# Cross-attention: the key and query fills for two batches ahead open an iteration, and the normalised input is turned one iteration earlier, at the end

## What is computed

```python
x = x + _L0_attn_ref(_layernorm(x), wq, wk, wv, wo)
# cross-attention, 16 heads of 16
q = _split_heads(_layernorm(x) @ Wq.T + bq)
k = _split_heads(ctx @ Wk.T + bk)
v = _split_heads(ctx @ Wv.T + bv)
scores = jnp.where(mask == 0, -jnp.inf, einsum('bhqd,bhkd->bhqk', q, k) / 4)
x = x + (merge(softmax(scores) @ v) @ Wo.T + bo)
x = x + _L0_ffn_ref(_layernorm(x), ...)
```

## Time and profile before

| | |
|---|---|
| median of 3 runs | 1809.52 us (1806.7 to 1829.16) |
| the profiled execution | 1793.75 us, of which its span 1791.8 us |
| mean granted TensorE clock of it | 0.924 |
| TensorE busy | 1543.1 us (86% of the span) |
| VectorE, ScalarE, GpSimd busy | 1053.8, 765.4, 427.1 us |
| the steps of the cross-attention | about 782 to 1375 us of the span |

### The profile page before, as it was taken

The page is one execution under the profiler, slowest core; times in us unless marked ns, Lnnn a source line. Parts: engine busy times, 40 slices in busy tenths (PEclk is TensorE's granted clock), DMA queues, the critical chain, the costliest instruction groups (busy, mean ns, idle before and its releaser), DMA issues. The chain is left out here.

```text
span 1791.8 us, 39290 instructions
## 1 busy us (share of the span) xinstructions
PE 1543.1 (86%) x12244; PEld 1335.2 (75%) x12244; DVE 1053.8 (59%) x2627; ACT 765.4 (43%) x1830; POOL 427.1 (24%) x564
## 2 busy tenths in 40 slices
PE   4799999999999999379889898989988606999998
PEld 3687878788888888367778787878876605888886
DVE  5658575767676666256566665666654314555553
ACT  4546464545555554135455554555543101222221
POOL 4202020202020303411222222222212062333332
PEclk9899999999999999679899998999886557999999
DMA  5603030302021111285666666566651052555552
GB/s 192 167 1 75 1 73 3 70 13 61 23 50 34 39 39 35 67 212 144 162 174 168 173 169 165 148 177 165 168 138 57 1 162 82 173 174 174 190 186 62
DMA packets 159949, 195.71 MB, mean 109 GB/s; under 512 B 83724, under 2 KB 128307, under 8 KB 159636
## 3 DMA queue, kind: packets, MB, share of 16 engines
q1 hardware_dynamic: 154356, 186.09, 38.1%
q0 software_dynamic: 3968, 6.59, 1.1%
q10 hardware_dynamic: 1568, 2.30, 0.4%
HBM read 138.63 MB, written 58.05 MB: 110 GB/s over the span
## 5 line engine op out<-in xcount | busy, mean ns | idle before, releaser
L1197 DVE TENSOR_REDUCE row_max<-psb_s 100x1 f32<-100x361 f32 x512 | 264.7, 531 | 201.8 <-PE psb_s L1340 200.1
L1090 ACT ACTIVATE probs<-psb_t 121x400 f32<-121x400 f32 (+1 forms) x384 | 193.6, 505 | 133.5 <-PE psb_t L1350 128.9
L1340 PE MATMUL psb_s<-k,q 97*100 97x362 f32 x512 | 193.1, 379 | 60.9 <-DMA k<-packed_keys 57.9
L419 POOL TENSOR_TENSOR diag<-neg_ident,row_max 100x400 fp32r<-100x400 f32 x128 | 112.2, 898 | 376.3 <-PE ps_t L666 204.5
L1350 PE MATMUL psb_t<-q,k 98*121 98x200 f32 (+1 forms) x768 | 161.7, 295 | 1.1 <-ACT probs L1090 1.0
L1340 PEld LDWEIGHTS psb_s<-k,q 97*100 97x100 f32 x512 | 91.4, 179 | 81.5 <-issue 52.1
L2027 PE MATMUL psd_y<-w_sb,hid 128*128 128x256 f32 x640 | 144.5, 379 | 0.0
L2019 PE MATMUL psd_h<-h_in,w_sb 128*128 128x256 f32 x640 | 142.9, 382 | 1.4 <-ACT h_in L1885 1.4
L1350 PEld LDWEIGHTS psb_t<-q,k 98*121 98x121 f32 (+1 forms) x768 | 135.7, 198 | 5.0 <-ACT probs L1090 1.8
L2019 PEld LDWEIGHTS psd_h<-h_in,w_sb 128*128 128x128 f32 x640 | 122.6, 192 | 18.6 <-issue 1.8
L2027 PEld LDWEIGHTS psd_y<-w_sb,hid 128*128 128x128 f32 x640 | 120.1, 190 | 15.5
(11 more groups left out here) (225 smaller groups left out, 3729.8 us busy)
## 6 DMA issues: line engine op xcount, KB each, us to landing
w_sb<-in_w SPq DMA_DIRECT2D x40, 1024.0 KB
packed_keys<-k_st SPq DMA_DIRECT2D x32, 724.0 KB, 3.6
k<-packed_keys SPq DMA_DIRECT2D x64, 362.0 KB
v_rows<-v_tok SPq DMA_DIRECT2D x32, 400.0 KB
v_ext<-v_rows SPq DMA_DIRECT2D x32, 400.0 KB
q<-packed_queries SPq DMA_DIRECT2D x64, 200.0 KB
k<-packed_keys SPq DMA_DIRECT2D x64, 181.0 KB
c_t<-in_contextT SPq DMA_DIRECT2D x32, 361.0 KB, 4.5
```

The costliest lines, as they stand in the source:

```text
L419: pool.tensor_tensor(diag[:, g % 2], c.neg_ident[0:S, 0:S].unsqueeze(1).to_broadcast([S, GH, S]), row_max[:, g // 2 % 2, g % 2].unsqueeze( ...
L1090: act.activation(probs[0:KT[kt], u % 2, kt], ps_t[i % 2][0:KT[kt], 0:4 * S], ACT.Exp, scale=HD2 ** -0.5).then_inc(probs_ready, 1)
L1197: dve.reduce_max(row_max[:, p, h:h + 1], ps_s[h % 2][0:S, 0:S2], AX_X).then_inc(max_ready, 1)
L1340: pe.matmul(ps_s[h % 2][0:S, 0:S2E], q2[0:97, p, u, g, S * a:S * (a + 1)], k2[0:97, p, u, g], start=True, stop=True).then_inc(scores_ready, 1)
```

## The change

In `step`, TensorE makes K0, Q0 and K1 of batch b + 2 behind the first, second and third shifted scores of the step, each ahead of the plain score that follows; they stood behind scores 2, 4 and `shifted(b, p, 1, 1)`. The turned maxima of the second half (MT1) move behind them, from behind the second shifted scores. The input is turned for batch b + 3 at the end of step b, behind `project`, instead of for b + 2 near its start. The order of the banks, the emptying on ScalarE and VectorE, and the start-up ahead of the steps follow. On VectorE the statistics of the input of b + 3 (`norm_stats`) move from behind head 1 to behind head 4. The code of the SP queue and of GpSimd stays as it is.

```diff
-        MT1, XT, K0, Q0, K1, V0, MT0, V1, V2 = range(9)
+        K0, Q0, K1, MT1, V0, MT0, V1, V2, XT = range(9)
...
-            return b + 1 if f in (MT0, V0, V1, V2) else b + 2
+            return b + 1 if f in (MT0, V0, V1, V2) else b + 3 if f == XT else b + 2
...
 # ScalarE, step
                 exps(b, 0, 0)
-                maxima(b, p, 1)
+                if more(b, 2):
+                    keys(b + 2, p, 0)
                 exps(b, 0, 1)
                 if more(b, 2):
-                    x_turned(b + 2, p)
+                    queries(b + 2, p)
                 exps(b, 0, 2)
                 if more(b, 2):
-                    keys(b + 2, p, 0)
+                    keys(b + 2, p, 1)
+                maxima(b, p, 1)
                 exps(b, 1, 0)
                 if not (isinstance(b, int) and b == 0):
                     raw_out(b - 1)
-                if more(b, 2):
-                    queries(b + 2, p)
                 exps(b, 1, 1)
-                if more(b, 2):
-                    keys(b + 2, p, 1)
                 exps(b, 1, 2)
...
                 exps(b, 3, 1)
+                if more(b, 3):
+                    x_turned(b + 3, p)
                 exps(b, 3, 2)
...
 # VectorE, step
                 if nxt:
-                    maxima(b + 1, 1 - p, 0, 2)
+                    maxima(b + 1, 1 - p, 0, 1)
+                if more(b, 2):
+                    keys(b + 2, p, 0)
+                if nxt:
+                    maxima(b + 1, 1 - p, 1, 2)
+                if more(b, 2):
+                    queries(b + 2, p)
+                if nxt:
+                    maxima(b + 1, 1 - p, 2, 3)
+                if more(b, 2):
+                    keys(b + 2, p, 1)
+                if nxt:
+                    maxima(b + 1, 1 - p, 3, 5)
                 if more(b, 3):
                     norm_stats(b + 3)
                 if nxt:
-                    maxima(b + 1, 1 - p, 2, 4)
-                if more(b, 2):
-                    keys(b + 2, p, 0)
-                if nxt:
-                    maxima(b + 1, 1 - p, 4, 5)
-                if more(b, 2):
-                    queries(b + 2, p)
-                if nxt:
-                    maxima(b + 1, 1 - p, 5, 6)
-                if more(b, 2):
-                    keys(b + 2, p, 1)
-                if nxt:
-                    maxima(b + 1, 1 - p, 6, 8)
+                    maxima(b + 1, 1 - p, 5, 8)
...
 # TensorE, step
                 shifted(b, p, 0, 0)
+                if next2:
+                    keys(b, p, 0)
                 maximum_of(0)
                 shifted(b, p, 0, 1)
+                if next2:
+                    queries(b, p)
+                maximum_of(1)
+                shifted(b, p, 0, 2)
+                if next2:
+                    keys(b, p, 1)
+                maximum_of(2)
                 turn_maxima(b, p, 1)
-                maximum_of(1)
-                if next2:
-                    turn_x(b, p)
-                shifted(b, p, 0, 2)
-                maximum_of(2)
                 if not first:
                     weighted(b - 1, 1 - p, 3)
-                if next2:
-                    keys(b, p, 0)
                 maximum_of(3)
                 shifted(b, p, 1, 0)
                 maximum_of(4)
-                if next2:
-                    queries(b, p)
                 shifted(b, p, 1, 1)
-                if next2:
-                    keys(b, p, 1)
                 maximum_of(5)
...
                     project(b - 1)
+                if more(b, 3):
+                    turn_x(b, p)
                 shifted(b, p, 3, 2)
```

More of the change, by code:

```diff
@@ L866, in bank_free @@
                 b, f = b - 1, f + FILLS
-            while isinstance(b, int) and b >= -2 and not exists(b, f):
+            while isinstance(b, int) and b >= -3 and not exists(b, f):
                 f -= 2
@@ L870, in bank_free @@
                     b, f = b - 1, f + FILLS
-            if not isinstance(b, int) or b >= -2:
+            if not isinstance(b, int) or b >= -3:
                 emptied(pe, b, f)
@@ L1104, in turned_out @@
                 ins.then_inc(ot_copied, 1)
-            x_turned(0, 0)
+            x_turned(0, 1)
             keys(0, 0, 0)
@@ L1109, in _ @@
             keys(0, 0, 1)
-            x_turned(1, 1)
+            x_turned(1, 0)
             keys(1, 1, 0)
@@ L1117, in _ @@
             values(0, 0, 2)
+            x_turned(2, 1)
             def step(b, p):
                 exps(b, 0, 0)
-                maxima(b, p, 1)
+                if more(b, 2):
+                    keys(b + 2, p, 0)
                 exps(b, 0, 1)
                 if more(b, 2):
-                    x_turned(b + 2, p)
+                    queries(b + 2, p)
                 exps(b, 0, 2)
                 if more(b, 2):
-                    keys(b + 2, p, 0)
+                    keys(b + 2, p, 1)
+                maxima(b, p, 1)
                 exps(b, 1, 0)
@@ L1226, in _ @@
             norm_stats(1)
+            normalize(1)
+            norm_stats(2)
             keys(0, 0, 0)
@@ L1229, in _ @@
             keys(0, 0, 1)
-            normalize(1)
+            normalize(2)
             keys(1, 1, 0)
@@ L1233, in _ @@
             keys(1, 1, 1)
-            norm_stats(2)
-            normalize(2)
             maxima(0, 0, 0, 16)
@@ L1386, in project @@
                 ins.then_inc(y_ready, 1)
-            turn_x(-2, 0)
+            turn_x(-3, 1)
             keys(-2, 0, 0)
@@ L1391, in _ @@
             keys(-2, 0, 1)
-            turn_x(-1, 1)
+            turn_x(-2, 0)
             keys(-1, 1, 0)
@@ L1401, in _ @@
             values(-1, 1, 2)
+            turn_x(-1, 1)
             for h in range(9, 16):
```

## The result

The changed kernel takes 1720.18 us (median of 4 runs, 1718.76 to 1721.74), the kernel before 1808.11 us (4 runs, 1806.37 to 1829.16): a ratio of 0.9537, interval 0.9495 to 0.9579. The ratios here leave slow runs out, so they are not the quotients of the medians. A later job on another chip, with 6 runs of it and 11 of the kernel before, gave 1717.75 against 1803.93 (ratio 0.9573, 0.9518 to 0.9629). The profiled executions stand 74 us apart: 1793.75 and 1719.54 us, spans 1791.8 and 1717.6.

The account below looks back on a forecast made before the run. TensorE plus one DMA wait a step was taken to bound the cross-attention. -53 (wait) + 16 (given back) - 26 (clock) = -63 us; from the median 1809.5 that is 1746.5, rounded to 1748; range 1725 to 1792.

Parts of the forecast that it names:

- Part 1: Cross-attention steps: fills moved ahead let the packed keys land with 2 us of slack; score 0's wait goes, 53.2 us off.
- Part 2: First half of a step: fills stand closer than ScalarE and VectorE empty them; 0.54 us a step, 16 us given back.
- Parts 3 and 4: Input turned at step's end: nobody waits; split context for K0, which opens the step: hidden by 0.28 us, taken as 0.
- Part 5: Placing DMA of half 1: lands 3.3 us after issue, wanted 3.4 us on; cost taken as 0.
- Part 6: TensorE's clock falls behind the long wait of a step: 26 of the 31 us taken as recovered.
- the sum: Profiled execution: -53 + 16 - 26 = -63 us, 1793.75 to 1731; 16 us carried over, 1746.5, rounded to 1748.
- Rival B: TensorE in a step's first half: the row of small waits keeps the clock falling; 1772 us, chance 0.17.

## Why the prediction was wrong

**What bounds the kernel, and that the wait goes** (Part 1): right. The view of waits names no pack, the stores begin at 4.02 us (4.2 walked), the keys' store at 6.71 (6.8), the pack at 10.6 (10.6). The run with two small loads puts the pack's landing at 4.9 us after its issue (5 walked) and the slack at 2.0 us (2 walked). The run of the old order without stores shows that nothing else of it cost anything: TensorE was at work for 470.75 of 479 us at a clock of 1.00.

**What is late next** (Part 2): right in place, too dear. K1 starts at 2.83 (2.94), score 5 at 6.02 (6.15), score 7 at 7.69 (7.86), shifted (2, 0) at 8.29 (8.47), the step takes 16.27 (16.46). Against the clean steps of the kernel before the mean step of 16.29 us gives back 0.35 us, 10 us in 30, instead of 0.54 and 16. The whole difference of the walked step is in its first half, 8.29 against 8.47; the second is 7.98, as walked. Score 7 was held by the statistics, but for 0.08 us instead of 0.26.

**Parts 3 and 4**: right. The turned input alone is worth nothing. The split for K0 must be there at 997.79; GpSimd's row of that step ends 0.26 us before, where 0.28 was walked (one step did wait for it, 0.3 us):

```profile
995.93 1.60 POOL L996 TENSOR_TENSOR c_lo<-c_t,c_hi 128x722 fp32r<-128x722 f32 x1
```

**The placed maxima** (Part 5): right that shifted (2, 0) doesn't wait; one step in 801 to 1280 us did, by 0.3. The last packets run 2.0 us after the issue and not 3.3. Where the DMA was waited for, the matmul started 0.35 us (without stores) and 0.8 us (with them) behind the last half microsecond with packets. So I put the slack in the changed kernel at 0.6 to 1.0 us of the 3.4 from issue to (2, 0), an estimate. Beyond that the delay is a jump: behind the keys' store the DMA takes 3.7 us till it is of use. The page "DMA: Bandwidth & Descriptors" of the Trainium skill ("Issuing engines are not separate DMA queues"), which I had weighed as speaking against the move, has the transfers of all issuing engines run on the same 16 DMA engines; the packet rows of the two placings agree. No row shows how the engines choose between the queues.

**The clock** (Part 6): right in kind, too small. I took 26 of 31 us; all of it came back, 1.00 from 801 us to the end of the steps. The clean steps bear the 31 out: 18.58 - 15.94 - 1.74 is 0.90 us a period, 25 in 28, where the sum had 0.92 and 26. Rival B had 0.17 and is out: waits of 0.2 us, and the cluster of them in each step, leave the clock alone. The Trainium skill ("TensorE: Matmul & The Clock Gate", "A second HAM failure mode: psum-queue depth-cycling") tells of short idles between groups of matmuls that kept a kernel's clock going down and up; that did not happen here.

**The step that failed** is the last of the sum: "That execution lies 16 us below the median of the runs, 1809.52; I carry the difference over". The sum took 16 us for something that the change leaves alone. By the runs with clocks (1.3 us for 0.001 of clock, correlation -0.97) it was the clock falls of the median run beyond those of the profiled one, and the change removes them as well: the profiled execution of the changed kernel lies 0.6 us below its median. The prediction's 1746.5 was then rounded up to 1748, another 1.5 us without a reason. By the sum without the 16, 1731, the miss would have been 11 us. Those 11 are three terms. In the 28 periods it is 9 us: the sum had 16.46 us and 0.18 of clock that stayed, and 16.32 was measured, so 4 us are the order's cost and 5 the clock. The end of the steps had 4 more, and the start and the rest 1 less each. The range inherited the error: its lower edge, 1725, is the median less 84; from the profiled execution it would have been 1710, and 1720 lies within it.

## What to carry to other kernels

- A wait that the profile puts at 1.7 us a step cost 2.7, because TensorE's clock fell behind it in some steps. Where a change removes such a wait, the spread between runs goes with it: start the sum from the run that is compared, and take the falls of the median run off as well, not only those of the profiled one.
- To advance a transfer, walk its whole chain from the engine that writes its source. Then walk every small DMA that others wait for against the large ones: here one issued 1.8 us ahead of a 724 KB store had its packets through 2.0 us later, one 0.15 us ahead 1.7 us later, and one 0.26 us behind it 3.0 us later, and all the gain of the change was gone.
- A step of a run in which the late wait was taken away is not the work of the step before: there another wait of 0.26 us came up that the long one had covered. Take the work from the clean steps of the kernel before, all of them.
- Two engines that fill and empty the same banks leave slack only in places. Moving one instruction showed the next wait each time: 3 us in two edits, and 28 and 90 us lost by the two after them.

## What the runs showed of the hardware that I had not expected

- The kernel before spreads over 38 us (1780 to 1818) in one job, with the granted clock from 0.933 to 0.903 in step with it. The changed kernel spreads over 4 us in its job (1716 to 1720, clock 0.943 to 0.946).
- The clock fell to half behind the long wait in 14 of 28 periods of the kernel before. The length of the wait did not decide it: it fell behind 1.40 us (at 1117.08) and stayed behind 2.00 (at 988.76). Waits of up to 1.1 us left it at 1.00, both in the run with two loads and, in 28 waits, in the run with the placing DMA behind the exponentials.
- A DMA of 3 KB from ScalarE's queue occupies ScalarE for 0.64 us of issue and 0.82 to 0.84 us to its next instruction; with it between the exponentials (1, 0) and the raw output's copy, a run was 31 us slower than the one that it was made from.
- The same DMA's packets ran 1.0 to 1.5 us after its issue with idle DMA engines (of use at 1.9), 1.0 to 2.0 us amid the query stores, 2.3 to 3.3 us amid the packs, and 2.5 to 3.0 us behind the keys' store (of use at 3.7).
